# Adjacency of the front issued together and masked in place, PSUM read-out of the scores ahead of the first block copy, other step tables, in a graph attention kernel

## The reference

```
h        = relu(layernorm(x))
neib_att = tanh(neigh @ Wn1 + bn1) @ Wn2 + bn2          # 4096 x 32
value    = neigh @ Wv + bv                              # 4096 x 128
x_att    = tanh(h @ Wx1 + bx1) @ Wx2 + bx2              # 4096 x 32
ws       = leaky_relu(x_att @ neib_att.T, 0.01)         # 4096 x 4096
ws       = softmax(where(adj > 0, ws, -9e15), axis=1)
out      = x + concat([h @ Wfx + bfx, ws @ value], 1)   # 4096 x 256
```

## Time and profile before

| | |
|---|---|
| median of 3 runs | 485.35 us (484.95 to 485.37) |
| profiled execution | 485.15 us, span 482.8 us |
| granted TensorE clock, mean | 0.998 |
| busy: PE, PEld | 464.3 us (96%), 424.5 us (88%) |
| busy: DVE, ACT, POOL | 427.7 (89%), 428.3 (89%), 258.4 us (54%) |
| chain that ended last | PE 75%, ACT 5%, issue 3%, DVE 3% |

### The profile page before, as it was taken

How to read it: one execution, slowest core, us unless ns; L and a number is a source line. 1 busy time by engine, 2 the same in 40 slices (tenths; PEclk the granted TensorE clock), 3 DMA queues, 4 the chain that set the end, 5 groups by cost and what they waited for, 6 DMA issues and landing times.

```text
span 482.8 us, 10844 instructions
## 1 busy us (share of the span) xinstructions
PE 464.3 (96%) x3728; PEld 424.5 (88%) x3728; DVE 427.7 (89%) x820; ACT 428.3 (89%) x714; POOL 258.4 (54%) x361
## 2 busy tenths in 40 slices
PE   8997789999999999999999999999999999999997
PEld 7975579998899899998999899999899899999896
DVE  3678899999999899989999999989999899999764
ACT  2464899999999999999999999999999999999973
POOL 3108247853677547945686557845686455454300
PEclk9999999999999999999999999999999999999999
DMA  8944635457555655557456654657457554553000
GB/s 303 304 88 90 153 67 89 81 90 163 106 88 93 130 118 100 100 90 157 93 88 109 131 110 91 109 99 159 79 95 139 91 88 79 108 100 56 11 12 12
DMA packets 32373, 51.51 MB, mean 107 GB/s; under 512 B 2368, under 2 KB 22976, under 8 KB 32320
## 3 DMA queue, kind: packets, MB, share of 16 engines
q0 software_dynamic: 9216, 33.56, 42.5%
q1 hardware_dynamic: 22816, 17.17, 11.0%
q10 hardware_dynamic: 288, 0.10, 0.2%
HBM read 80.19 MB, written 4.19 MB: 175 GB/s over the span
## 4 chain that ended last, share of the span: by engine, by line
PE 75%; ACT 5%; issue 3%; DVE 3%; POOLq 0%; POOL 0%; DVEq 0%; ACTq 0%
PE ps_turned L922 20%; PE ps_product L943 11%; PE ps_product L945 11%; PE ps_product L944 11%; PE ps_scores L900 10%; PE ps_scores L899 6%; PE ps_product L865 3%; ACT scores L561 3%; ACT pt_hi L523 2%; DVE scores L706 2%; PE ps_product L857 1%; PE ps_product L841 1%; ACT scores L549 1%; PE ps_product L848 1%; PE ps_product L954 1%
## 5 line engine op out<-in xcount | busy, mean ns | idle before, releaser
L453 POOL TENSOR_TENSOR scores<-scores,mask 128x512 f32<-128x512 f32 x117 | 136.4, 1166 | 116.9 <-ACT scores L549 116.3
L688 DVE TENSOR_TENSOR pt_lo<-ps_turned,pt_hi 128x512 fp32r<-128x512 f32 x256 | 173.9, 685 | 20.8 <-PE ps_product L945 9.8
L523 ACT ACTIVATE pt_hi<-ps_turned 128x512 fp32r<-128x512 f32 x256 | 158.1, 618 | 20.9 <-PE ps_turned L922 20.3
L943 PE MATMUL ps_product<-pt_hi,v_hi 128*128 128x256 f32 x512 | 164.9, 322 | 0.1
L922 PE MATMUL ps_turned<-ident,scores 128*128 128x128 f32 x1024 | 153.8, 273 | 0.8 <-DVE pt_lo L688 0.6
L561 ACT ACTIVATE scores<-scores,low_top 128x1024 f32<-128x1024 f32 x128 | 151.5, 1183 | 0.0
L945 PE MATMUL ps_product<-pt_lo,v_hi 128*128 128x256 f32 x512 | 144.5, 282 | 0.0
L944 PE MATMUL ps_product<-pt_hi,v_lo 128*128 128x256 f32 x512 | 144.0, 281 | 0.0
L549 ACT ACTIVATE scores<-ps_scores 128x1024 f32<-128x1024 f32 x128 | 133.3, 1041 | 9.6 <-PE ps_scores L900 9.4
L922 PEld LDWEIGHTS ps_turned<-ident,scores 128*128 128x128 f32 x1024 | 121.9, 140 | 17.7 <-issue 2.0
L706 DVE CUSTOM_DVE_ANT_0 scores<-ps_scores,scores,low_top 128x1024 f32<-128x1024 f32 x96 | 122.5, 1276 | 0.9 <-ACT scores L549 0.4
(11 more groups left out here) (70 smaller groups left out, 359.8 us busy)
## 6 DMA issues: line engine op xcount, KB each, us to landing
adj_in<-in_adj POOLq DMA_DIRECT2D x60, 512.0 KB, 5.4
scores<-in_neigh_t SPq DMA_DIRECT2D x8, 512.0 KB, 7.9
x_rows<-in_x SPq DMA_DIRECT2D x7, 512.0 KB, 5.9
x_left<-in_x SPq DMA_DIRECT2D x8, 256.0 KB, 5.7
x_right<-in_x SPq DMA_DIRECT2D x16, 128.0 KB, 5.3
scores<-in_adj POOLq DMA_DIRECT2D x4, 512.0 KB, 6.4
out_h<-x_left SPq DMA_DIRECT2D x8, 256.0 KB, 2.3
out_h<-x_right SPq DMA_DIRECT2D x16, 128.0 KB, 2.1
```

The costliest lines, as they stand in the source:

```text
L453: pool.tensor_tensor(half, half, mask[:, s % MASK_RING, BANK:CHUNK], ALU.add).then_inc(masked, 1)
L523: act.activation(pt_hi[:, (2 * b + u) % HI_RING], pt[:, u], ACT.Copy).then_inc(hi_done, 1)
L688: dve.tensor_tensor(pt_lo[:, u], pt[:, u], pt_hi[:, (2 * b + u) % HI_RING].bitcast(FP32), ALU.subtract).then_inc(lo_done, 1)
L943: pe.matmul(product_of(g), v_hi[:, block, :], high, start=block == 0, stop=False)
```

## The change

- Filler transposes: `FILL` goes from (6, 6, 6, 4, 0...) to (6, 0, 0, 0...): 16 fewer. The 15 at the very start stay.
- POOL issues all four front loads in a row as soon as the last neighbour block has landed; the wait for `x_ahead` there goes.
- DVE masks the front in place: `front_mask(p)` turns two chunks (128x2048) of `adj_front` at once, at steps 0, 2, 3 and 6, in `x_work`. The eight single masks of these chunks go, and the ring numbering of masks skips the front (`ring_place`). PE and POOL read the mask through `mask_of_chunk`.
- ACT's step now begins with `rise(s)`, ahead of `hi(s, 0)` and `aggregate(s)`. This holds in all steps.
- DVE's step runs `neigh_rest` (low part of the late values) behind `lo(s, 1)` instead of ahead of `x_work`.
- The tables of the `x` work change, in every group (see the diff). `WIDE_0` moves the left product of group 0 from step 1 to step 0.

```diff
-FILL = (6, 6, 6, 4, 0, 0, 0, 0)
+FILL = (6, 0, 0, 0, 0, 0, 0, 0)
-X_LOAD = -12
-X_STATS = (-6, -6, -6, -4)
-X_AGGR = -2
-X_RSTD = (-2, -2, -1, 0)
-X_NORM = (1, 3, 3, 4)
+X_LOAD = -7
+X_STATS = (-6, -6, -5, -4)
+X_AGGR = -3
+X_RSTD = (-2, -2, -2, 0)
+X_NORM = (1, 3, 3, 5)
-X_WIDE, X_LEFT = (15, 17, 19, 19), 19
-X_LEFT_LOAD, X_SUM = 8, (13, 18)
-X_RIGHT = 14
+X_WIDE, X_LEFT = (16, 17, 18, 19), 19
+X_LEFT_LOAD, X_SUM = 7, (9, 17)
+X_RIGHT = 15
-WIDE_0 = 1
+WIDE_0 = 0
+FRONT_MASKS = (0, 2, 3, 6)
@@ POOL, ahead of its step loop
             pool.wait_ge(rows_in[NEIGH_GROUPS - 1], 16)
-            load_adj(2 * LOAD)
-            pool.wait_ge(x_ahead_in, 16)
-            load_adj(3 * LOAD)
+            for p in range(FRONT // LOAD):
+                load_adj(ADJ_RING + p * LOAD)
             for i in range(NEWTON + 1):
                 rstd_of(1, i)
-            load_adj(4 * LOAD)
-            load_adj(5 * LOAD)
@@ ACT
             def step(s):
+                rise(s)
                 hi(s, 0)
                 aggregate(s)
-                rise(s)
                 hi(s, 1)
@@ DVE
+            def front_mask(p):
+                dve.wait_ge(front_ready[p], 16)
+                pair = adj_front[:, p * LOAD:(p + 1) * LOAD, :].rearrange("p a n -> p (a n)")
+                dve.tensor_scalar(pair, pair, 0.0, MASKED, ALU.is_le, ALU.mult).then_inc(front_masked, 1)
@@ DVE, x_work(s)
+                for p in range(FRONT // LOAD):
+                    if s == FRONT_MASKS[p]:
+                        front_mask(p)
@@ DVE, step(s)
                 close(s)
-                neigh_rest(s)
                 x_work(s)
                 lo(s, 1)
+                neigh_rest(s)
@@ PE, score(s, h)
-                    pe.wait_ge(mask_done, k + 1)
+                    if made_in_front(s):
+                        pe.wait_ge(front_masked, (s - ADJ_RING) // LOAD + 1)
+                    else:
+                        pe.wait_ge(mask_done, ring_place(s) + 1)
```

More of the change, by code:

```diff
@@ L200, in build @@
         front_ready = [sem(f"front_ready{i}") for i in range(FRONT // LOAD)]
-        mask_done = sem("mask_done")
+        mask_done, front_masked = sem("mask_done"), sem("front_masked")
         scored = sem("scored")
@@ L273, in right_due, with ring_place, made_in_front, mask_of_chunk @@
             return b // ASTEPS + 2 if b >= 0 and b % ASTEPS == 0 and b // ASTEPS < AGROUPS - 2 else None
+        def ring_place(n):
+            return n - FRONT if n >= ADJ_RING else n
+        def made_in_front(n):
+            return ADJ_RING <= n < ADJ_RING + FRONT
+        def mask_of_chunk(n):
+            return adj_front[:, n - ADJ_RING, :] if made_in_front(n) else mask[:, ring_place(n) % MASK_RING, :]
         def chunk_of(s):
@@ L440, in step @@
                 if s % LOAD == 0 and n < STEPS and not ADJ_RING <= s < ADJ_RING + FRONT:
-                    pool.wait_ge(mask_done, s + LOAD)
+                    pool.wait_ge(mask_done, ring_place(s) + LOAD)
                     load_adj(n)
@@ L452, in step @@
                     half = scores[:, parity * TILES + tile, c * CHUNK + BANK:(c + 1) * CHUNK]
-                    pool.tensor_tensor(half, half, mask[:, s % MASK_RING, BANK:CHUNK], ALU.add).then_inc(masked, 1)
+                    pool.tensor_tensor(half, half, mask_of_chunk(s)[:, BANK:CHUNK], ALU.add).then_inc(masked, 1)
                 for i in range(NEWTON + 1):
@@ L538, in rise @@
                 if s == GSTEPS:
-                    act.wait_ge(mask_done, ADJ_RING + FRONT)
+                    act.wait_ge(masked, ADJ_RING + FRONT - POOL_MASKS)
                 if s == (TILES - 1) * CHUNKS:
@@ L664, in mask_of @@
             def mask_of(n):
[L666 to L677, removed]
+                if made_in_front(n):
+                    return
+                r = ring_place(n)
+                dve.wait_ge(adj_ready[r % ADJ_RING // LOAD], 16 * (r // ADJ_RING + 1))
+                if r >= MASK_RING:
+                    gone = r - MASK_RING
+                    if gone >= ADJ_RING:
+                        gone += FRONT
+                    dve.wait_ge(scored, gone + 1)
+                    if gone >= POOL_MASKS:
+                        dve.wait_ge(masked, gone + 1 - POOL_MASKS)
+                dve.tensor_scalar(mask[:, r % MASK_RING, :], adj_in[:, r % ADJ_RING, :], 0.0, MASKED, ALU.is_le,
                                   ALU.mult).then_inc(mask_done, 1)
+            def front_mask(p):
+                dve.wait_ge(front_ready[p], 16)
+                pair = adj_front[:, p * LOAD:(p + 1) * LOAD, :].rearrange("p a n -> p (a n)")
+                dve.tensor_scalar(pair, pair, 0.0, MASKED, ALU.is_le, ALU.mult).then_inc(front_masked, 1)
             def lo(s, u):
@@ L898, in score @@
                 if not on_pool:
-                    pe.matmul(ps[:, s % 2, half], ident_bf16, mask[:, s % MASK_RING, half], start=True, stop=False)
+                    pe.matmul(ps[:, s % 2, half], ident_bf16, mask_of_chunk(s)[:, half], start=True, stop=False)
                 last = pe.matmul(ps[:, s % 2, half], xs[:, parity, tile * P:(tile + 1) * P],
```

## The result

| | median | runs | ratio to before, 95% interval |
|---|---|---|---|
| before | 485.31 us (484.77 to 485.37) | 5 | |
| changed | 479.41 us (478.98 to 482.48) | 5 | 0.9898 [0.9875, 0.9921] |

The change gains 5.9 us, and the time lies 0.9 us under the low end of the forecast range (482.9, 480.3 to 486.4). For the front I therefore also show a second profiled execution of the same kernel (run `again`, span 476.8), and for stretches differences between two points of one execution.

What follows compares the result with a forecast made beforehand. PE was taken to bound the regular period, no engine the front. From 485.15 us, the front's -1.2 and ACT order's -1.25 gave 482.7, plus 0.2 for the median: 482.9 us, range 480.3 to 486.4.

Steps and rivals of the forecast that it cites:

- ACT's new order: In regular periods ACT reads out scores while waiting for a turn; 0.25 us a period, 1.25 us over five.
- PE's three holds: In a regular 16-step period PE's weight loads were held three times, 1.0 us together; only one was counted as shortened.
- all holds go: Rival, chance 0.14: all holds of PE in the regular periods vanish, 5 us and the front's 1.2 gained; 479.2 us.
- Range of steps: The gain from ACT's order was counted in five regular periods only, at 0.25 us each.
- Fillers: Neighbour rounds 2 and 3 shorten by 0.66 and 0.43 us, so step 0's scores start 1.09 us earlier.
- Front loads and pair masks: In the front, POOL's 1.21 us of issue moves and masks take 0.9 less; 1.2 us kept at the front's end.
- Pair mask: DVE's 2048-column mask in the front: 0.8 us each, 3.2 for four; the first eats 0.8 of 1.09 us.
- 1.73 us of DVE's wait: DVE's wait at 48.55 us for POOL's sum of the left half, claimed to shrink to about 0.5 us.
- Tables: Steps of the `x` work: same instructions at other steps, each hidden beside PE's own queue; costed at nothing.
- Clock rival: Rival, chance 0.03: without fillers PE's clock falls to 1.2 GHz for one neighbour round, adding 3.45 us; 486.4 us.
- Late rows: Rival, chance 0.20: group 2's rows land late, hold DVE 1 to 2 us, eat the front's 1.2; 484.7 us.

Runs made afterwards that it cites:

- b_rise: Kernel before with one edit, ACT's `rise` moved ahead of `hi(s, 0)` and the aggregation; 479.47 us, ratio 0.9881.
- b_nofill: Kernel before with only the 16 filler transposes taken out; 484.11 us, ratio 0.998.
- a_fill: Changed kernel with the 16 filler transposes put back; 480.62 us, ratio 0.9904.
- f_front: Kernel before with the front's edits alone (loads, pair masks, `WIDE_0`, `neigh_rest`), keeping its fillers, ACT order and `x` tables; 484.84 us, ratio 0.9992.
- a_oldtab: Changed kernel with all `x` tables back at their old steps; 478.27 us, ratio 0.985.
- t_wide: Changed kernel with fillers (6, 6, 0, 0) and only the wide products back at their old steps; 477.40 us, ratio 0.9839.
- t_sum: Changed kernel with fillers (6, 6, 0, 0) and only POOL's sums and the left half's load at their old steps; 479.21 us, ratio 0.9876.
- t_right: Changed kernel with fillers (6, 6, 0, 0) and only the right product back at its old step, 14; 479.47 us, ratio 0.9884.

## Why the prediction was wrong

**Direction and place of the gain** were right; the size was off in three terms, and the largest of them puts the time outside the range.

- **ACT's new order: counted 1.25 us, measured 5.7 alone.** This is the step that failed. I took one of PE's three holds, as the others "follow DVE, which the order does not shorten". All three went, and 0.8 us a period rather than 0.25. What I called a separate cause was the same one: DVE itself waited 1.0 us for `hi` and 0.6 for ACT's exponential in the period of before, and 0.6 and 0.4 in that of `b_rise`. The rows I had could have warned me: of ACT's 2.1 us of idle time in the period 2.0 were waits for turns, so nearly all the time that it could win lay there. My rival "all holds go", 479.2 us, had the mechanism, and I gave it 0.14. That its time is that of the measured 479.4 is in part luck: the order and the fillers gave more than its 6.2 us, and the tables, counted at nothing, took the surplus back.
- **Range of steps.** I counted five regular periods. The order also gave 0.5 us up to step 12 (where `b_rise` stands 0.8 ahead, 0.3 of it from the start) and 0.8 from 12 to 28, where ACT waits for turns as well.
- **Fillers: counted 1.09, of which the first pair mask eats 0.8.** Measured 1.14 us at the first score, and 1.0 still there at the end (`b_nofill`). Whether the pair mask eats part of it beside the front's edits is less clear. The medians of `a_fill` and `again` differ by 0.6 us, with three of the six times of `again` 1.6 to 2.9 us above its fastest. The profiled executions differ by 1.5 us at step 0 and 1.7 at step 12 and 1.8 at the end, with a fall of the clock in `a_fill` (39 to 43 us). Neither shows a loss of 0.8.
- **Front loads and pair masks: counted as most of 1.2 us, measured 0.4** (`f_front`, against a ratio that can't tell it from none). The 1.73 us of DVE's wait, which I expected at 0.5, stayed at 1.76: POOL came 0.3 us earlier, and DVE, with fewer masks, as much earlier. Fillers and front together came to 1.5 us against the 1.2 of the sum; its parts did not come out.
- **Pair mask: 0.69 us against 0.8 taken and bounds of 0.51 to 1.02.** The mean of 0.51 for a single was itself misread: seven take 0.42 to 0.54 and one takes 1.02 beside POOL's sums (49.16 in the timeline of before).
- **Tables: counted at nothing, measured +1.8 to +2.1 us** (`a_oldtab` against `again`, `t_wide` against `t_sum` and `t_right`), 0.24 to 0.33 a period and 0.3 behind the last. "Each hides beside PE's own queue" was wrong for the wide products: the one in step 15 stood in a hole of PE.
- **Clock rival (0.03, +3.45 us).** Half speed in the first rounds happened, in some executions: 3.26 us in the profiled one, where PE had not yet reached the full clock, and 1.6 in `a_oldtab`, where it fell back. I had looked only at whether the fuller rounds would keep the level, not at whether the first two rounds, between waits for DMA, reach it. And the earlier trace rows was one execution: the granted clock that read 1.00 in it between 36 and 41 us fell in half of the profiled executions with the new front. That filler transposes "save nothing" there was right of the time and wrong of what they do.
- **Late rows (0.20).** The wait exists, 0.24 to 0.56 us in most executions and 1.08 at most, and `again` has the same lead on both sides of it.

The medians add up: order -5.7, fillers -1.1, front -0.4, wide products +1.8 to +2.1, sum -5.1 to -5.4, and the two measured medians of the change lie 5.9 and 5.1 us under before. They differ by 0.65 us from one timing to the other, so the sum is no closer than that.

## What to carry to other kernels

Ask of every engine in the loop what its idle time is spent on, not only of the busiest one. Work and waits of any engine add up to the period, so the sum proves nothing. But an engine whose waits are nearly all for one predecessor, and which has work at hand that does not need it, can be given that work first. Here the trial was one moved line, and it paid 5.7 us where the one hold on the chain promised 1.25. Before moving an instruction of the bound engine to another step, look whether its old place was a hole. Before taking out work that "costs nothing", look at what it keeps up, by several executions and their spread, not by one. And where a clock column reads full speed, compare the durations of like instructions too.

## What was not expected of the hardware

- POOL's issue of the changed kernel's four front loads, which stand in a row in its list:
```profile
16.58 0.53 POOL L429 DMA_DIRECT2D scores<-in_adj  x1 [0.73 <-DMA scores<-in_neigh_t]
21.22 0.54 POOL L429 DMA_DIRECT2D scores<-in_adj  x1 [4.11 <-issue]
24.17 0.53 POOL L429 DMA_DIRECT2D scores<-in_adj  x1 [2.41 <-issue]
26.89 0.53 POOL L429 DMA_DIRECT2D scores<-in_adj  x1 [2.20 <-issue]
```
  "All at once" is not what happens: POOL is held 2.2 to 4.1 us ahead of each further load while earlier ones are under way. It costs nothing here, since POOL's next instruction waits for DVE's statistics until 38.84 us; that it is the number of loads outstanding was not tried.
- A mask of 128x2048 takes 0.69 us where one of 128x1024 takes 0.42. If the rest grows with the width, 0.15 us of each is fixed, an estimate from these two (twice 0.42 less 0.69): a pair saves 0.15 us.
